# A transformer layer and a recurrent layer on one core: the first layer's attention by groups of four heads

## What is computed

```python
H, NH, HD = 512, 16, 32
def attention(q, k, v, mask):
    scores = einsum('bhqd,bhkd->bhqk', q, k) / sqrt(HD)
    scores = scores * mask - 10000.0 * (1.0 - mask)
    probs = softmax(scores, axis=-1)
    return einsum('bhqk,bhkd->bhqd', probs, v)

# layer 0, for each of the 8 batch entries (256 tokens, 512 channels):
h = layernorm(x);  q, k, v = split(h @ w_qkv + b_qkv)
x = x + merge(attention(q, k, v, self_mask)) @ w_ao + b_ao
h = layernorm(x);  q = h @ w_q + b_q;  k, v = split(enc @ w_kv + b_kv)
x = x + merge(attention(q, k, v, cross_mask)) @ w_co + b_co
h = layernorm(x)
x = x + gelu(h @ w1 + b1) @ w2 + b2          # w1: 512 x 2048, w2: 2048 x 512
# layer 1: x = recurrent_layer(x, state), with enc's entries as its states
```

## Time and profile before

| what | us |
|---|---|
| median of three runs | 2486.43 |
| the profiled execution | 2493.44 |
| its span, first to last instruction | 2491.7 |
| PE busy | 2119.6 (85%) |
| DVE busy | 1479.9 (59%) |
| ACT busy | 887.6 (36%) |
| POOL busy | 526.3 (21%) |
| mean granted clock of PE | 0.905 |

### The profile page before, as it was taken

The page is one execution under the profiler, slowest core; times in us unless marked ns, Lnnn a source line. Parts: engine busy times, 40 slices in busy tenths (PEclk is TensorE's granted clock), DMA queues, the critical chain, the costliest instruction groups (busy, mean ns, idle before and its releaser), DMA issues. The chain is left out here.

```text
span 2491.7 us, 31238 instructions
## 1 busy us (share of the span) xinstructions
PE 2119.6 (85%) x11012; PEld 1429.4 (57%) x11012; DVE 1479.9 (59%) x2431; ACT 887.6 (36%) x2029; POOL 526.3 (21%) x248
## 2 busy tenths in 40 slices
PE   6789999999999999999978488588887979787555
PEld 4466666666666666665645266465655656565332
DVE  2454453543534535445241128989898989999961
ACT  2356354453554545535441121141413132321212
POOL 0222131231222312213120112132222222222000
PEclk9699999999999999999978788698989889898778
DMA  5101202111122121120212622414131314131210
GB/s 182 43 14 60 94 23 85 60 56 68 56 77 76 40 85 57 60 93 5 100 45 84 193 77 77 130 41 135 51 120 49 127 42 135 43 119 51 86 51 9
DMA packets 130861, 186.60 MB, mean 75 GB/s; under 512 B 23352, under 2 KB 71224, under 8 KB 130728
## 3 DMA queue, kind: packets, MB, share of 16 engines
q1 hardware_dynamic: 113832, 168.04, 20.6%
q10 hardware_dynamic: 16896, 16.80, 2.0%
HBM read 147.05 MB, written 37.77 MB: 74 GB/s over the span
## 5 line engine op out<-in xcount | busy, mean ns | idle before, releaser
L304 POOL TENSOR_TENSOR a_prob<-a_prob,a_rowinv 128x1024 f32<-128x1024 f32 x128 | 242.6, 1895 | 835.5 <-DVE a_rowinv L737 835.5
L944 ACT ACTIVATE a_prob<-a_score,a_low 128x256 f32<-128x256 f32 x512 | 253.8, 497 | 397.0 <-DVE a_low L730 396.9
L1662 DVE TENSOR_TENSOR_SCAN b_ring<-b_ws,b_ring 128x1028 f32<-128x1028 f32 x128 | 351.6, 2787 | 3.0
L722 DVE SCALAR_TENSOR_TENSOR a_score<-a_S,a_mask 128x1024 f32<-128x1024 f32 x128 | 156.7, 1224 | 181.4 <-PE a_S L454 166.4
L357 PE MATMUL a_G<-a_hTf,a_ring 128*128 128x256 f32 x1024 | 244.3, 394 | 8.9 <-issue 3.5
L368 PE MATMUL a_G<-a_ring,a_f1T 128*128 128x512 f32 x512 | 234.8, 600 | 3.0 <-DVE a_xf L709 1.9
L1439 POOL TENSOR_TENSOR b_mixed<-b_mixed,b_xaT 128x1024 f32<-128x1024 f32 x40 | 130.1, 3258 | 478.3 <-DVE b_mixed L1679 478.3
L357 PEld LDWEIGHTS a_G<-a_hTf,a_ring 128*128 128x128 f32 x1024 | 198.7, 198 | 52.1 <-issue 22.9
L730 DVE CUSTOM_DVE_ANT_0 a_score<-a_score,a_fill 128x256 f32<-128x256 f32 x512 | 207.2, 460 | 18.4 <-DVE a_score L722 0.2
L467 PEld LDWEIGHTS a_PT<-a_ident,a_prob 128*128 128x128 f32 x1024 | 125.7, 147 | 59.5 <-issue 31.5
L1537 PE MATMUL b_y_bank<-b_ring,b_same_quad 128*32 128x128 f32 x2048 | 80.6, 305 | 91.6 <-DVE b_ring L1669 91.6
(11 more groups left out here) (157 smaller groups left out, 3266.4 us busy)
## 6 DMA issues: line engine op xcount, KB each, us to landing
a_ring<-in_w_dram SPq DMA_DIRECT2D x64, 1024.0 KB, 5.2
b_vs<-b_v_all SPq DMA_DIRECT2D x32, 512.0 KB, 5.0
b_w_all<-b_wT ACTq DMA_DIRECT2D x8, 514.0 KB, 3.3
b_ws<-b_w_all SPq DMA_DIRECT2D x8, 514.0 KB, 3.3
a_x_new<-in_x_dram SPq DMA_DIRECT2D x8, 512.0 KB, 3.7
a_enc<-in_enc_dram SPq DMA_DIRECT2D x8, 512.0 KB, 4.2
x_all<-a_xf SPq DMA_DIRECT2D x8, 512.0 KB, 3.3
b_xa<-x_all SPq DMA_DIRECT2D x8, 512.0 KB, 4.4
```

The lines of the kernel that those rows point to most:

```text
L304: nc.gpsimd.tensor_tensor(pair, pair, inv.to_broadcast([P, 2 * TT, SEQ]), ALU.mult)\
L722: nc.vector.scalar_tensor_tensor(out=score[:, :, :], in0=S[:, :, :], scalar=-SCORE_SCALE, in1=mask[:, at:at + 1, :].to_broadcast([P, 2, TT ...
L944: last = nc.scalar.activation(prob[:, 2 * (i % 2) + u, a * SEQ:(a + 1) * SEQ], score[:, u, a * SEQ:(a + 1) * SEQ], ACT.Exp, bias=low[:, 2 ...
L1662: last = nc.vector.tensor_tensor_scan(x_, flat(ws[:, :, :]), x_, 0.0, ALU.mult, ALU.add)
```

## The change

Heads are handled in groups of four instead of pairs, and the PSUM banks are shared out anew: S has four banks (four heads) instead of two, PT one (one head) instead of two, O one as before, and G two instead of three.

- `scores(b, at, g)` computes four heads, one in each of the four row tiles.
- `turn_probs` and `take_probs` handle one head each, so 32 turns and 32 copies take the place of 16 and 16 in an iteration; `exponential` also goes by head.
- `mask_scores`, `invert` and `normalize` still handle pairs. `score` has four slots instead of two, `prob` eight instead of four.
- With two banks for the projections the order of `G_TILES` is another, and with it the order of all queues. `FF_STEPS` now has the second-layer quarter 0 ahead of the first-layer quarter 1.
- Two waits at once (for data and for a bank) become one where they are for the same semaphore (`reads` in `claim`).

```diff
-        score = sb("score", P, 2, TT * SEQ)
-        prob = sb("prob", P, 4, TT * SEQ)
+        score = sb("score", P, 4, TT * SEQ)
+        prob = sb("prob", P, 8, TT * SEQ)
...
-        S = psum("S", 2, TT * SEQ)
-        PT = psum("PT", 2, 2 * SEQ)
+        S = psum("S", HPG, TT * SEQ)
+        PT = psum("PT", 2 * SEQ)
         O = psum("O", 512)
-        G = [psum(f"G{i}", 512) for i in range(3)]
+        G = [psum(f"G{i}", 512) for i in range(2)]
...
+        G_TILES = [XK, XK, XV, CO, CO, XV, HT3, HT3, F1, F1, F2, F2, F1, F1, F1, F1, ENCT, F2, ENCT, F2, F1, AO, AO,
+                   F1, F2, HT2, HT2, F2, XQ, XQ, F2, HT1, F2, HT1, Q, Q, K, K, V, V]
+        BANK = [n % len(G) for n in range(len(G_TILES))]
...
-        FF_STEPS = [(1, 0), (1, 1), (2, 0), (1, 2), (2, 1), (1, 3), (2, 2), (2, 3)]
+        FF_STEPS = [(1, 0), (2, 0), (1, 1), (1, 2), (2, 1), (1, 3), (2, 2), (2, 3)]
...
             def iteration(b, streams, before):
-                for i in range(3):
+                for i in range(4):
                     normalize(b, 0, i)
                 if "ff" in streams:
                     begin_ff(b - 1)
                 pool.wait_ge(x_in.sem, x_in.at(b, 1))
                 add_bias(xb[:, :], 0, x_new[:, :]).then_inc(xb_made.sem, 1)
-                for i in range(3, NP):
+                for i in range(4, NP):
                     normalize(b, 0, i)
...
+            def scores(b, at, g):
...
                 for a in range(TT):
-                    for u in range(2):
-                        rows = slice((2 * i % HPG + u) * HD, (2 * i % HPG + u + 1) * HD)
+                    for j in range(HPG):
+                        rows = slice(j * HD, (j + 1) * HD)
+                        last = nc.tensor.matmul(S[:, j, a * SEQ:(a + 1) * SEQ], qT[rows, at, g, a * P:(a + 1) * P],
+                                                kT[rows, at, g, :], start=True, stop=True)
...
+            def turn_probs(b, at, head):
+                n = at * NH + head
+                pe.wait_ge(prob_made.sem, prob_made.at(b, n // 2 + 1))
+                pe.wait_ge(pt_taken.sem, pt_taken.at(b, n))
...
+                if ff:
+                    fill.ff2(d, 3, 0)
+                if more:
+                    fill.hidden_in(b + 1, 0)
+                if ff:
+                    fill.ff2(d, 3, 1)
+                if more:
+                    fill.hidden_in(b + 1, 1)
...
+                mask_scores(b, 0, 6)
                 take_context(b, 0, 1)
+                mask_scores(b, 0, 7)
+                if ff:
+                    take_ff2(d, 0, 0)
+                invert(b, 0, 6)
+                invert(b, 0, 7)
+                if ff:
+                    take_ff2(d, 0, 1)
...
+            def exponential(b, at, head, first=False):
...
+                act.wait_ge(low_made.sem, low_made.at(b, n + 1))
+                for a in range(TT):
+                    last = nc.scalar.activation(prob[:, head % 8, a * SEQ:(a + 1) * SEQ],
+                                                score[:, head % 4, a * SEQ:(a + 1) * SEQ], ACT.Exp,
...
+            def take_probs(b, at, head):
+                act.wait_ge(pt_full.sem, pt_full.at(b, at * NH + head + 1))
+                act.wait_ge(o_full.sem, o_full.at(b, at * CG + head // HPG))
+                nc.scalar.activation(probT[:, head % 4, :], PT[:, :], ACT.Copy).then_inc(pt_taken.sem, 1)
```

More of the change, by code:

```diff
@@ L176, in g_emptied, with g_free @@
             return g_taken[st, who].sem, g_taken[st, who].at(d, tiles_upto(n, st, who))
-        def g_free(b, streams, before, name, k):
+        def g_free(streams, before, name, k):
             n = place[name][k]
-            for turn, present, upto in ((b, streams, n), (b - 1, before, ALL + 1)):
+            for back, present, upto in ((0, streams, n), (1, before, ALL + 1)):
                 for m in reversed(range(upto)):
-                    st, other, _ = G_TILES[m]
-                    if BANK[m] == BANK[n] and st in present:
-                        return g_emptied(turn + SHIFT[st], other, place[other].index(m))
+                    if BANK[m] == BANK[n] and G_TILES[m][0] in present:
+                        return back, m
             return None
@@ L433, in ff1 @@
                     w1 = self.weights(d, 1, quarter)
-                    if quarter == 0 and k == 0:
-                        pe.wait_ge(*g_emptied(d, "hT3", 1))
-                    self.project_T("f1", 2 * quarter + k, w1, k * 2 * P, hTf)
+                    self.project_T("f1", 2 * quarter + k, w1, k * 2 * P, hTf,
+                                   reads=("hT3", 1, 0) if quarter == 0 and k == 0 else None)
                 def ff2(self, d, quarter, a, parts=range(PARTS)):
                     w2 = self.weights(d, 2, quarter)
-                    if a == 0 and 0 in parts:
-                        pe.wait_ge(*g_emptied(d, "f1", 2 * quarter + 1))
@@ L561, in iteration @@
                 if ff:
-                    fill.ff2(d, 1, 1)
-                    fill.ff1(d, 3, 0)
+                    fill.ff1(d, 3, 1)
+                    fill.ff2(d, 2, 0)
                 fill.hidden_cross(b, 0)
@@ L566, in iteration @@
                 if ff:
-                    fill.ff1(d, 3, 1)
+                    fill.ff2(d, 2, 1)
                 fill.cross_q(b, 0)
@@ L623, in iteration @@
-                scores(b, 1, 7)
-                contexts(b, 1, 2)
-                if more:
-                    fill.self_v(b + 1, 1, HALVES[0])
-                turn_probs(b, 1, 6)
-                if more:
-                    fill.self_v(b + 1, 1, HALVES[1])
+                if more:
+                    fill.hidden_in(b + 1, 1)
+                scores(b, 1, 1)
+                for head, (k, half) in enumerate(((0, 0), (0, 1), (1, 0), (1, 1))):
+                    if more:
+                        fill.self_q(b + 1, k, HALVES[half])
+                    turn_probs(b, 1, head)
@@ new lines, in iteration @@
+                scores(b, 1, 2)
+                contexts(b, 1, 0)
+                for head, (k, half) in enumerate(((0, 0), (0, 1), (1, 0), (1, 1))):
+                    if more:
+                        fill.self_k(b + 1, k, HALVES[half])
+                    turn_probs(b, 1, 4 + head)
+                scores(b, 1, 3)
+                contexts(b, 1, 1)
+                for head, (k, half) in enumerate(((0, 0), (0, 1), (1, 0), (1, 1))):
+                    if more:
+                        fill.self_v(b + 1, k, HALVES[half])
+                    turn_probs(b, 1, 8 + head)
@@ L649, in _ @@
             last = Filler(BATCH, ("ff",), ("ff", "main"))
-            turn_probs(d, 1, NP - 1)
-            contexts(d, 1, CG - 1)
+            contexts(d, 1, 2)
+            for head in range(12, NH):
+                turn_probs(d, 1, head)
+            contexts(d, 1, 3)
             for k in range(TT):
@@ L1057, in _ @@
             d = BATCH - 1
-            take_probs(d, 1, NP - 1)
+            for head in range(12, NH):
+                take_probs(d, 1, head)
             root(d, "ff")
```

391 lines of the change are left out of this document (185 added, 206 removed).

## The result

The changed kernel takes 2546.89 us (median of four runs, 2544.42 to 2548.60), the kernel before on the same chip 2485.89 (2484.34 to 2486.92): a ratio of 1.025, 95% interval 1.0237 to 1.0263. The prediction was 2514 in a range of 2480 to 2534: slower was right, and half of the loss was missed, 61 us where 28 were forecast.

What follows compares the result with a forecast made beforehand. PE was taken to bound the inner iterations, a chain through all engines the first and last cross attention. First iteration -11, inner +34, last +7.5, tail -1 gave +29.5 us; less 2 for rounding, 2514 us, range 2480 to 2534.

Steps and rivals of the forecast that it cites:

- the start of the iteration: Start of an inner iteration: PE would idle 0.1 us there.
- the last cross attention: Last iteration's cross attention, up to the output projection: would go from 56.94 to 50 us.
- the step from the trace to the median: Whole kernel: the median was taken to lie 7 us below the profiled execution, as before, giving 2516 us.
- The scores: Score blocks of four heads on PE: 1.06 us each, saving 9.5 us an iteration with fewer changes of array shape.
- Rival 3: Scores on PE: four row tiles give no more than two, 2555 us; chance 0.05.
- hT3: Feed-forward's turned hidden state: PE waits for h, DVE's copy of v and ACT's evacuation, 6.8 us where 2.4 was.
- ff1(1,1): Feed-forward's first layer: PE waits 2.75 us for the bank of ff2(0,1), 3.5 together with the contexts' 0.77.
- hT2: Feed-forward: hT2's first half waits 1.25 us for the bank of ff1(3,1), ff2(2,1) waits 0.7; together 2.0.
- ff2: Cross attention's start: ff2(3,1) waits 0.7 us for its bank, PE's second turn 1.5; together 2.3.
- rivals 1 and 2: Inner iterations: 1, feed-forward waits shrink, about 2468 us, chance 0.12; 2, POOL blocks DVE less, 2480 to 2490, 0.13.
- The clock: Inner iterations: falls behind the feed-forward's waits cost 3.9 us an iteration for 1.5 before, +2.4.
- The first iteration and the tail: First iteration's attention: -11 us, with one pass of scores per four heads; feed-forward tail: -1 us.

Runs made afterwards that it cites:

- before_two_banks: The kernel before with two projection banks instead of three, its old order of tiles kept: 2504.92 us, 20 more than before.
- six moves: The changed kernel with four operations moved in its queues, and ACT's copies of turned heads ahead of exponentials at two more places: 2460.45 us, 0.9908 of before.

## Why the prediction was off

The direction and the mechanism held: PE saves 9 us an iteration and waits longer than that. Four sizes of the sum failed: what a stall costs beyond its idle time (put at nothing, about 2 us an iteration), the start of the iteration (0.1 for 2.2), the last cross attention (50 for 55.35), and the step from the trace to the median (7 us).

*The scores: right.* A block of four heads takes 1.07 us (335.51 to the contexts at 336.58), 1.06 was predicted. Worked out from the distances between the starts of PE's records at full clock, PE's own work fell by 9.1 us an iteration (9.5 predicted). Rival 3 is out: two tiles took 1.06 us for half the work. The Trainium skill ("TensorE: Matmul & The Clock Gate", section "Measured speedup vs the span model") gives 3.07 times for four row tiles. The 0.26 us a block that this would add, by the prediction's estimate, don't show: 1.07 for 1.06. How four tiles compare with a single one no run here measures.

*The waits at hT3, ff1(1,1), hT2 and ff2: right by place and cause, a little too large.* 2.91 + 2.6 + 0.35 us at hT3 (6.8 predicted), 2.58 + 0.76 at ff1(1,1) and the contexts (3.5), 0.54 (0.7), 1.09 + 0.77 at hT2 (2.0), 0.44 + 1.22 at cross attention's start (2.3). Together 13.2 of a predicted 15.3. Two were taken out on the chip and a third cut to a quarter (26, 24 and 14 us), and all stand in every iteration, so rivals 1 and 2, in which they shrink by themselves, fell.

*The clock: right in sum, not in its parts.* It fell for 6.83 us behind hT3 in every iteration, and for 3.41 behind ff1(1,1) in every one, where half of them were expected; three more falls stood around the start of an iteration. The records whose distance doubled cost about 3.8 us an iteration, 1.4 before: +2.4, as predicted.

*"Start of the iteration: 0.1": the wait that was wrong.* DVE comes 3.2 to 3.6 us late out of the loop's jump. This stood in the trace of before and wasn't read, because there nothing waited for it: I added operations up along each queue and took the jump for free. With copies by the head, one of them is queued behind the exponential that waits for DVE, and PE waits 1.8 to 2.2 us in four of six iterations; with PE's own gap that is 2.2 us a mean iteration. The written-out loop gave back 2.3. In size this error was covered: the other waits came 2.1 us below what was predicted, so the idle time of an inner iteration, 15.6 us, is the predicted 15.4, by luck.

*The price of a stall: put at nothing, and the step that made the inner sum too small.* The sum took a stall to cost its idle time and no more. Between the rows at 339.85 and 343.54 lie 3.69 us, between those at 344.03 and 345.76, the same work without a wait, 1.73. So this stall cost 1.96, and the idle column says 1.79. The difference fits an array that has to be filled again; the rows show its size, not its cause. Over some twelve stalls an iteration that is about 2 us which idle times don't show: counted by starts, the waits grew by about 15.0 us, while idle time grew by 13.1, where 12.8 was predicted. (The prediction set 2.6 us of old idle time against its 15.4; its trace has 2.4.) The sum is -9.1 + 15.0 + 2.4 and 0.3 of rest = +8.6, where -9.5 + 12.8 + 2.4 = +5.7 was predicted; six times 2.9 is 17 us of the miss.

*The last cross attention: a term too small.* 50 us predicted, 55.35 measured. The prediction shows no working for its 50, and its turn of 0.44 us is one at the higher clock level. PE ran at a mean granted clock of 0.69 there, at 0.50 from 1344.8 us on, and each turn through the one bank of turned probabilities took 1.87 us with its copy. How much of the 5 us is the clock and how much the bank no run separates:

```profile
1354.50 1.09 PE L461 MATMUL a_PT<-a_ident,a_prob 128*128 128x128 f32 x4 [0.78 <-ACT a_probT L926]
1356.37 1.09 PE L461 MATMUL a_PT<-a_ident,a_prob 128*128 128x128 f32 x4 [0.78 <-ACT a_probT L926]
```

*The first iteration and the tail: right* (-11.5 and -1.1 for -11 and -1), but not the 2.5 us ahead of the first scores. Their cause is open: two banks alone don't bring them (the first scores of before_two_banks start at 45.9), and over the variants of the changed kernel they start at 47.0 to 48.6.

*From the trace to the median.* The prediction took the changed kernel's profiled execution to stand 7 us above its median, as that of before did. It stood level, and no trace shows where those 7 us lie. Another 2 us were taken off for rounding, without need. So the miss of 33 us is 17 to 18 for the inner iterations, 6.5 for the last one (1.1 of it in self attention), 2 for the start, 7 and 2 for these two steps, less 2 for the recurrent layer, which the prediction took as unchanged.

## What to carry over

When an operation is cut into smaller ones, look at each in-order queue for what now stands between the pieces and could wait: one copy behind an exponential, or one take-out behind a reciprocal, cost PE a quarter or so of all that the change saved. Such stalls can be found in a walk through the queues and are cheap to mend: six moves made 86 us, and turned a kernel that lost 2.5% into one that wins 0.9%. In that walk a loop's jump is an operation with a duration: read it from the trace of before on each engine, as "issue" time and from the branch's own record, also where nothing waits for it yet. And count each stall of PE a little above its idle time.

## What was not expected of the hardware

- A jump back left DVE idle for 2.4 to 4.2 us in this kernel, wherever PE's own gap didn't cover it (from its branch to the next instruction of its queue lie 2.7 to 5.0 us in all thirteen looped kernels); ACT and POOL needed 0.2 us or less. PE's branch took 0.2 us at some jumps, with no packet on q8 there, and 3.8 to 6.0 us at others, with packets. The two kernels with the old orders had the slow branch at every jump and no gap, since PE's queue reached it some 4 us ahead of the array. The Trainium skill ("Runtime: NRT & Kernel Launch", section "Instruction fetch mechanics") says that a taken branch whose target isn't held forces a DMA fetch before execution goes on. PE's slow branches, each with packets, agree; that PE goes through whole iterations of 1,700 instructions without a packet shows that its target is held at the others. What decides between the two is open.
- Whether a wait stands ahead of an activation table's load or behind it is worth 1.28 us on the chain. In the kernel before, that came with the removal of all jumps, which cost 21 us in all.
- Taking out a stall of 2.6 us in each of seven iterations gave 24 to 26 us, not 18. In both kernels the clock's falls went or shrank with it: its mean over the inner iterations rose from 0.96 to 0.97 and 0.98.
